# The first layer's attention as one stream of 64 head pairs, with scores formed twice and banks of their own for each use

## What is computed

```python
x = x + layernorm(attn(layernorm(x)))          # 32 heads of 16, one shared key/value head
x = x + layernorm(layernorm(x) @ W.T + bias)   # 512 x 512, W dequantised

q = (h @ Wq).reshape(b, s, 32, 16)
k, v = (h @ Wkv)[..., :16], (h @ Wkv)[..., 16:]
scores = einsum('bqhd,bkd->bhqk', q, k) * 0.25 + slopes[h] * (pos[k] - pos[q])
attn = softmax(where(k <= q, scores, -inf))
out = einsum('bhqk,bkd->bqhd', attn, v).reshape(b, s, 512) @ Wo
```

## Time and profile before

| what | value |
|---|---|
| median of 3 runs | 2521.51 us (2521.39 to 2526.22) |
| the profiled execution's own time | 2520.12 us |
| its span, first to last instruction | 2518.3 us |
| busy in the span: PE, DVE, ACT, POOL | 85%, 74%, 61%, 27% |
| granted TensorE clock, mean | 0.94 |
| the first layer in the span | from 59 us to 824 us |
| before it: weights' preparation | 0 to 59 us |
| after it: the second layer | 824 to 2518 us |

### The profile page before, as it was taken

How to read it: one execution, slowest core, us unless ns; L and a number is a source line. 1 busy time by engine, 2 the same in 40 slices (tenths; PEclk the granted TensorE clock), 3 DMA queues, 4 the chain that set the end, 5 groups by cost and what they waited for, 6 DMA issues and landing times. The chain is left out here.

```text
span 2518.3 us, 49756 instructions
## 1 busy us (share of the span) xinstructions
PE 2146.9 (85%) x18352; PEld 1310.3 (52%) x18352; DVE 1864.5 (74%) x4645; ACT 1531.5 (61%) x3606; POOL 688.4 (27%) x563
## 2 busy tenths in 40 slices
PE   6688777778774589999999999999999999758997
PEld 2465555555552255555555555655555556423443
DVE  3688897897995477777777777777777777575554
ACT  2587776777771376667667676667666767341221
POOL 0312212111110243343433343334333333112221
PEclk9899899889997799999999999999999999978999
DMA  5101001000000343444334434443344333320000
GB/s 203 33 2 35 1 7 47 2 18 18 2 18 17 115 81 63 89 87 91 80 66 89 81 71 82 80 91 78 64 89 84 66 68 65 72 87 17 34 17 34
DMA packets 380593, 147.59 MB, mean 59 GB/s; under 512 B 354928, under 2 KB 359664, under 8 KB 378304
## 3 DMA queue, kind: packets, MB, share of 16 engines
q1 hardware_dynamic: 380352, 144.41, 25.5%
HBM read 48.95 MB, written 11.53 MB: 24 GB/s over the span
## 5 line engine op out<-in xcount | busy, mean ns | idle before, releaser
L1157 ACT ACTIVATE xp<-xp,nm 128x128 f32<-128x128 f32 (+3 forms) x512 | 281.3, 550 | 354.5 <-DVE nm L1236 354.5
L1017 POOL TENSOR_TENSOR q_in_sbuf<-q_in_sbuf,sinq 128x512 f32<-128x512 f32 x128 | 231.2, 1806 | 688.2 <-ACT q_in_sbuf L1145 581.3
L1207 DVE SCALAR_TENSOR_TENSOR probs_lo<-xp,rl,probs_hi 128x128 f16<-128x128 f32 (+3 forms) x512 | 263.5, 576 | 109.4 <-ACT probs_hi L1122 109.4
L575 ACT ACTIVATE xp<-xp,nm 128x512 f32<-128x512 f32 (+3 forms) x512 | 249.8, 569 | 50.9 <-DVE nm L680 49.1
L680 DVE CUSTOM_DVE_ANT_0 xp<-bank,tab,cs 128x512 f32<-128x512 f32 (+3 forms) x512 | 250.2, 545 | 4.3 <-PE bank L459 2.0
L1236 DVE CUSTOM_DVE_ANT_0 xp<-bank,mask,cs 128x128 f32<-128x128 f32 (+3 forms) x512 | 250.3, 545 | 0.0
L1122 ACT ACTIVATE probs_hi<-xp,rl 128x128 f16<-128x128 f32 (+3 forms) x512 | 244.0, 549 | 0.7 <-DVE rl L1256 0.7
L472 PE MATMUL bank<-ident,xp 128*128 128x128 f32 x1280 | 182.7, 291 | 62.6 <-ACT xp L575 45.6
L1041 PE MATMUL bank<-xT_hi,wq_hi 128*128 128x512 f16 x512 | 195.2, 381 | 43.2 <-DVE yacc L1251 37.4
L708 DVE TENSOR_TENSOR pT_lo<-bank,pT_hi 128x384 f16<-128x384 f32 (+1 forms) x384 | 207.1, 593 | 32.5 <-ACT pT_hi L543 32.4
L1041 PE MATMUL bank<-p1T_hi,v_hi 128*128 128x128 f16 x1280 | 223.0, 220 | 2.9 <-DMA p1T_lo<-probs_lo 2.9
(11 more groups left out here) (235 smaller groups left out, 5535.9 us busy)
## 6 DMA issues: line engine op xcount, KB each, us to landing
raw_q<-in_wq SPq DMA_DIRECT2D x8, 1024.0 KB, 5.3
raw_o<-in_wo SPq DMA_DIRECT2D x8, 1024.0 KB, 5.6
x_front<-in_x SPq DMA_DIRECT2D x4, 1024.0 KB, 5.8
xb<-in_x SPq DMA_DIRECT2D x4, 1024.0 KB, 7.1
x_scratch<-xb SPq DMA_DIRECT2D x4, 1024.0 KB, 4.4
x_before<-x_scratch SPq DMA_DIRECT2D x4, 1024.0 KB, 5.6
wup<-in_wup SPq DMA_DIRECT2D x3, 1024.0 KB, 11.9
fused_scratch<-fused SPq DMA_DIRECT2D x12, 256.0 KB, 2.4
```

The source lines that it names most:

```text
L575: act.activation(x, x, ACT.Exp, scale=-1.0, bias=nm[:, h % 4, t:t + 1]).then_inc(s_ex, 1)
L1017: pool.tensor_tensor(qs[:, i % 2, :], qs[:, i % 2, :], rope["sink" if u[0] == "k" else "sinq"][:, :], ALU.mult).then_inc(s_rot, 1)
L1157: ins = act.activation(x, x, ACT.Exp, scale=-1.0, bias=nm[:, m % 3, t:t + 1], accum_out=ls[:, m % 3, t:t + 1])
L1207: ins = dve.scalar_tensor_tensor(pr[1][:, m % 2, c], xp[:, m % 3, c], rl[:, m % 3, t:t + 1], pr[0][:, m % 2, c], ALU.mult, ALU.subtract)
```

## The change

`layer0` becomes one block without barriers: a list of steps, one per pair of heads, for all 64 pairs of the four batches (`STEPS`). Step n of each engine forms the scores of pair n, the exponents of pair n - 6, weighs the values of pair n - 8 and norms the heads of pair n - 9; `FRONT` and `BACK` say at which steps of a batch its input norm, its projections and its back end are done.

- The scores are formed twice on PE. Once with queries in the partitions (`scores`, banks 0 to 2), of which DVE only takes the maximum (`maximise`, five `tensor_reduce` of 512 columns per pair). The second time with keys in the partitions (`exponents`, banks 3 to 5), so that the weights need no transposes. Slopes times positions and minus the maxima are extra rows of the stacked operands (`qs`, `ks`), and the mask is a small product (`far` x `tri`) added to each diagonal tile.
- ACT takes the exponential from PSUM to `px`, five instructions of 512 columns per pair. POOL makes the high halves of the five blocks (`weights_hi`, L487, a cast) and the low halves of two blocks; DVE makes the low halves of three (`weights_lo`, L888). All of these read SBUF, no longer PSUM.
- The queries' stacks are made by SP with 24 DMAs for each group of four pairs (`stack_queries`), the maxima's rows with 4 DMAs (`stack_maxima`).
- A head's output is summed and divided on POOL (`norm_heads`, four small instructions per pair). The normalised rows are made on ACT (`normalise`), the additions of the residual on POOL (`add_rows`), whose `rstd` has two more instructions.
- All other uses share banks 6 and 7. The tables `sel` and `pairmask` are no longer loaded.

The core of the diff (the new functions of POOL and of DVE; the removed lines are those printed above):

```diff
+        STEPS = range(-20, NP + N_LAG + 26)
+        FRONT = {"load": -16, "norm": -11, "n1": (-8, -7), "V": -6, "K": -5}
+        BACK = {"load": 27, "o": (14, 17, 21, 26), "y": (28, 28, 29, 29), "add1": 30, "n2": (32, 34),
+                "f": (36, 36, 38, 38), "add2": 39, "n3": (46, 47)}
...
+        groups = {"s": banks[0:3], "x": banks[3:6], "rest": banks[6:8]}
...
+                def rstd(i):
+                    pool.wait_ge(s_ve, i + 1)
...
+                    pool.tensor_tensor(rs[:, :], ve[:, :], C["mhalf"][:, 0:TT], ALU.pow).then_inc(s_pw, 1)
+                    pool.wait_ge(s_pw, 2 * i + 1)
+                    pool.tensor_tensor(nb[:, :], mv[:, :, 0], rs[:, :], ALU.mult).then_inc(s_pw, 1)
+                    pool.wait_ge(s_pw, 2 * i + 2)
+                    pool.tensor_scalar(nb[:, :], nb[:, :], -1.0, None, ALU.mult).then_inc(s_rs, 1)
...
+                def weights_hi(p):
+                    if p >= 2:
+                        pool.wait_ge(s_pf, p - 1)
+                    for i, (c0, c1) in enumerate(((0, 2), (2, 4), (4, 5))):
+                        pool.wait_ge(*emptied[("x", p, c1 - 1)])
+                        pool.tensor_copy(ph[0][:, p % 2, c0:c1, :], px[:, p % 2, c0:c1, :]).then_inc(s_wh, 1)
+                    pool.wait_ge(s_wh, 3 * p + 3)
+                    pool.tensor_tensor(ph[1][:, p % 2, 3:5, :], px[:, p % 2, 3:5, :], ph[0][:, p % 2, 3:5, :],
+                                       ALU.subtract).then_inc(s_wc, 1)
...
+                for n in STEPS:
+                    if 0 <= n - X_LAG < NP:
+                        weights_hi(n - X_LAG)
+                    if 0 <= n - N_LAG < NP:
+                        norm_heads(n - N_LAG)
+                    for u in norms_at(n):
+                        rstd(norm_no[u])
+                        if u in add_no:
+                            add_rows(u)
...
+                def turn(n, *which):
+                    for i in which:
+                        if 0 <= n < NP:
+                            scores(n, i)
+                        if 0 <= n - X_LAG < NP:
+                            exponents(n - X_LAG, i)
...
+                    for u in norms_at(n):
+                        normalise(u)
...
+                def weights_lo(p, i):
+                    c = slice(2 * i, 2 * i + 2 - i)
+                    dve.wait_ge(s_wh, 3 * p + i + 1)
...
+                    dve.tensor_tensor(ph[1][:, p % 2, c, :], px[:, p % 2, c, :], ph[0][:, p % 2, c, :],
+                                      ALU.subtract).then_inc(s_wl, 1)
```

More of the change, by code:

```diff
@@ new lines, in layer0 @@
+        kk = [sc.sb("k_hi", [P, S], F16), sc.sb("k_lo", [P, S], F16)]
+        kb = sc.sb("k_both", [P, 2, S], F16)
+        kz = sc.sb("k_stack_max", [P, 2, 2, S], F16)
+        ks = sc.sb("k_stack", [P, 2, 2, S], F16)
+        posr = sc.sb("position_rows", [P, S], F16)
+        v2 = sc.sb("v2", [P, 2, TT, 2 * EV], F16)
+        px = sc.sb("weights", [P, 2, 5, S])
+        ph = [sc.sb("weights_hi", [P, 2, 5, S], F16), sc.sb("weights_lo", [P, 2, 5, S], F16)]
+        pos = px[:, 1, 0, :]
+        sl = px[:, 1, 1, 0:H0]
@@ new lines, in layer0 @@
+        s_vd = sc.sem("s_values_out")
+        s_qf = sc.sem("s_queries_filled")
+        s_qh = sc.sem("s_queries_hi")
+        s_qd = sc.sem("s_queries_out")
+        s_qs = [sc.sem(f"s_queries_stacked{i}") for i in range(2)]
+        s_sf = sc.sem("s_scores_filled")
+        s_sd = sc.sem("s_scores_maximised")
+        s_mx = sc.sem("s_maxima")
+        s_mf = sc.sem("s_maxima_transposed")
+        s_mh = sc.sem("s_maxima_hi")
+        s_md = sc.sem("s_maxima_out")
+        s_mr = [sc.sem(f"s_maxima_stacked{i}") for i in range(2)]
@@ L251, in layer0 @@
+        s_ff = sc.sem("s_f_filled")
+        s_fd = sc.sem("s_f_out")
         s_out = sc.sem("s_x_stored")
[L253 to L269, removed]
@@ new lines, in layer0 @@
+        fillings = {"s": [], "x": [], "rest": []}
+        for n in STEPS:
+            if 0 <= n < NP:
+                fillings["s"] += [("s", n, i) for i in range(5)]
+            if 0 <= n - X_LAG < NP:
+                fillings["x"] += [("x", n - X_LAG, i) for i in range(5)]
+            if 0 <= n - V_LAG < NP:
+                fillings["rest"].append(("pv", n - V_LAG))
+            if n % GP == 0 and 0 <= n // GP - 1 < NG:
+                fillings["rest"].append(("m", n // GP - 1))
+            fillings["rest"] += others(n)
@@ new lines, in layer0, with bank_of @@
+        for u in fillings["s"] + fillings["x"] + fillings["rest"]:
+            full, empty = signals[u[0]]
+            counted[full] = counted.get(full, 0) + 1
+            filled[u], emptied[u] = (full, counted[full]), (empty, counted[full])
+        def bank_of(u):
+            k, i = place[u]
+            return groups[k][i % len(groups[k])]
+        norms, adds = [], []
+        for n in STEPS:
+            for kind, when in (("n1", FRONT["norm"]), ("a1", BACK["add1"]), ("n2", BACK["add1"] + 1),
+                               ("a2", BACK["add2"]), ("n3", BACK["add2"] + 1)):
+                if at(n, when) is not None:
+                    norms.append((kind, at(n, when)))
+                    if kind in ("a1", "a2"):
+                        adds.append((kind, at(n, when)))
@@ new lines, in statistics, with variance @@
+                def statistics(t, src):
+                    ch.tick(dve.bn_stats(st[:, int(src is xf), t, :], src[:, t, :]))
+                def variance(u):
+                    if norm_no[u]:
+                        dve.wait_ge(s_nm, TT * norm_no[u])
+                    ch.settle()
+                    for t in range(TT):
+                        ch.tick(dve.bn_aggr(mv[:, t, :], st[:, int(u[0] == "n1"), t, :]))
+                    ch.settle()
+                    dve.tensor_scalar(ve[:, :], mv[:, :, 1], EPS, None, ALU.add).then_inc(s_ve, 1)
```

998 lines of the change are left out of this document (558 added, 440 removed).

## The result

The changed kernel takes 2558.1 us in the median of four runs (2555.0 to 2566.2), the kernel before 2522.3: a ratio of 1.0145, 95% interval 1.0122 to 1.0167. It is slower, by 36 us. The forecast was slower by 100, that is 2620 us, with a range of 2430 to 2740. The profiled execution of the change is the longest of its four (2566.2 us, span 2564.4), so between the two profiled executions there are 46 us to explain.

The account below looks back on a forecast made before the run. POOL, with the time of the port it shares with DVE, was taken to bind: 131 start + 627 pairs + 100 batch work + 66 end = 924 us against 824, so 2620 us from 2520.1; range 2430 to 2740.

Parts of the forecast that it names:

- POOL with gaps in which it waits for ACT's exponentials: Sign that the forecast is wrong: POOL would stand idle for ACT's exponentials, or for PE's sums.
- POOL over 85% busy: Sign that the forecast is right, in the layer's middle: POOL busy or waiting for itself or for DVE's low halves.
- A plain pair: Pair of heads without per-batch work: 8.2 us of POOL plus 1.6 of port, 9.8 us; 64 of them 627.
- Where it waits for its own last instruction, 0.25 us pass: POOL's waits for itself: five of eight instructions 1.2 us, the other starts 0.25 together, per pair.
- POOL's work per batch: Five rstd 10 us, residual additions 12.4, norms 11: together 33 us per batch, 100 for three batches.
- the bubble at the norms: Three norms per batch where ACT waits for POOL, then makes rows and exponentials before POOL's next cast: 3.7 us each.
- Start: Layer's beginning: stack of queries ready at 107 to 112, then six scores-only steps; POOL starts at 131 us.
- 3.3 us each: Time of each of the first six steps, which form scores only, before POOL starts.
- 6 us: Layer's end: the last pair's way through DVE, PE, ACT and DVE to POOL, before a back end of 60 us.
- POOL is cheap and DVE binds: Rival: POOL's pair costs 6.5 us, DVE binds at 8.2 per pair, kernel faster at 2418 us; chance 0.26.
- Small instructions are dear: Rival: POOL's small instructions near 1.02 us, norm_heads 2.7 us more per pair, kernel at 2793 us; chance 0.12.
- The port costs nothing: Rival: the shared port's time is nothing or falls into waits, 102 us less, 2518 us, no change; chance 0.12.

Follow-up runs that it names:

- Experiment 3: Changed kernel with ACT's normalised rows and POOL's residual additions one step later, and n2, n3 too: 2500.3 us, ratio 0.9903 to the kernel before.
- experiment 12: Changed kernel with 12 of the first query stack's 24 DMAs issued by ACT's queue: 2557.4 us, ratio 1.0117 to the kernel before.
- experiment 1: Changed kernel with DVE's low halves replaced by one-input reductions of the same columns, leaving out three blocks' low halves: 2508.0 us, ratio 0.9938 to the kernel before.
- experiment 2: Changed kernel with the low half of one block on POOL instead of two, four on DVE: 2538.6 us, ratio 1.0062 to the kernel before.

## Why the prediction was wrong in size

For the plain pair the side and the mechanism were right: POOL binds, DVE has room, the port's time lies on POOL. For the rest they were not. The prediction wrote down "POOL with gaps in which it waits for ACT's exponentials" and PE's low clock as signs that it is wrong, and both are there: 116.5 us of such gaps, and a clock of 0.50 in the keys' step. Of its signs of being right, POOL over 85% busy became 78%, DVE under 75% became 76%, and DVE waits for `weights_hi` for 10.6 us in all. The size was 2.2 times too large by the profiled executions (100 against 46 us), 2.8 times by the medians (36). By steps:

- **A plain pair, 9.8 us foreseen, 7.55 measured; 144 us too much over 64.** The step that failed most is "Where it waits for its own last instruction, 0.25 us pass", five times a pair and 0.25 more for other starts: 1.45 us. In the plain step above, POOL's instructions follow one another within 0.08 us or overlap: 0.1 us in place of 1.45, which is 87 of the 144 us. The 0.26 of the earlier trace rows is the gap between two instructions of the second layer, 512 columns each; it was the only such row I took, and it isn't the price of a wait for oneself in general (even behind the power of a norm the gap is 0.07). Why it is longer there, no run shows. The rest: casts 2.69 for 3.1 (512 columns 0.605, not the table's 0.70; the fixed part, 2 x 0.605 less 1.04, is 0.17 where 0.2 was taken), the low half 2.12 for 2.35, small instructions 1.2 for 1.3, the port 1.45 for 1.6. Measured parts: 2.69 + 2.12 + 1.2 + 1.45 and 0.1 of gaps are 7.55.
- **POOL's work per batch, 100 foreseen, 150 measured** (633 less 64 x 7.55). The prediction had the bubble at the norms as 3.7 us each; it is 7.7 where the rows above show it, because ACT loses its lead and POOL waits at the two next casts too. Experiment 3 takes most of this away and with it 58 us. Nothing was priced for the steps in which DVE makes the next keys: two of them last 17.7 us, PE stands 5.55 us behind DVE, and its clock falls to its lower level.
- **Start, 131 foreseen, 147 measured.** The steps that failed are "3.3 us each" for the six steps of scores alone, and a smaller one ahead of them. The first scores started at 114.8, where the stack was to be ready at 107 to 112: the first query's low half came at 97.6, not 93, and the 24 issues then took 0.63 us each, near the upper end of the prediction's 0.4 to 0.67 (experiment 12). From the first maxima to POOL's first cast 31.9 us pass, 5.3 for each of six steps. DVE's reductions there are 34, about 22 us, 3.7 a step, and between them DVE waits for PE's products, which I had priced at nothing:

```profile
L874 DVE TENSOR_REDUCE mx<-bank 128x1 f32<-128x512 f32 x14 | 8.9, 679 | 12.2 <-PE bank L544 12.2
```

- **End, 66 foreseen, 86 measured.** The step that failed first is "6 us" for the last pair's way to POOL's normed heads. They were finished 14.3 us after the last low half, at 794.5, because POOL, in order, made an `rstd` and the four residual additions of the batch before ahead of them, and PE stood 11.02 us for them:

```profile
788.23 4.93 POOL L499 TENSOR_TENSOR xb<-xb,yb 128x512 f32<-128x512 f32 x4 [0.93 <-ACT yb L707]
794.60 1.11 PE L588 MATMUL bank<-ident,heads_normed 128*128 128x128 f32 x4 [11.02 <-POOL heads_normed L478]
```

  That is 8 of the 20 us. In experiment 3, where `rstd` stands among the heads and the additions behind them, the same way takes 7.5 us (727.65 to 735.2). In the change ACT also makes that norm's four rows, 2.93 us, before it copies the heads' transposes. The other 12 us aren't divided by an experiment; PE's clock over the stretch is 0.69.
- **The rivals.** "POOL is cheap and DVE binds" put its bound at 8.2 us for POOL's pair and would have had the change faster. POOL came to 7.55, under that bound, and the kernel is still slower: the rival's start and end were as far off as mine, and it had nothing for the long steps. "Small instructions are dear" is out (0.295). "The port costs nothing" is out by experiment 1. That it put the time at no change, 36 us from what was measured, would have been an accident of other terms.

The sum of the four: -144 + 50 + 16 + 20 = -58 of the layer, and +4 of the second: 100 - 54 = 46. Two errors of opposite sign, each larger than the answer of 46 itself, stood in a forecast whose direction was right. The range held the measured time for that reason, by luck and not by its working. Taking nine of the eleven long steps away without touching POOL's work is what turns the change into a gain (2500 us).

The Trainium skill, SBUF — State Buffer, section on who interferes with whom, has a DVE instruction with two SBUF inputs and a GpSimd one that reads SBUF locking each other out for the whole instruction. The timeline of the plain step and experiment 1 agree: 1.4 us per plain pair, 50 us in all.

## What to carry to other kernels

Price a step of an engine that takes over work as the sum of its instructions alone and measure the gaps between them from neighbours of the same kind, not behind one odd instruction. Then look at the steps that are not plain: an in-order engine that waits for a result made at the end of its partner's step loses its lead over that partner, and a delay of one step at that point was worth more (58 us) than moving a block of work from one engine to another (19 us). Where two engines share a port, moving a block from one to the other gives back part of what it takes, so a split is worth little near the balance.

## What the runs showed of the hardware

- A cast from f32 to f16 on POOL takes 1.04 us for 1024 columns and 0.605 for 512; two inputs of 1024 columns take 2.12, and 64 columns 0.295. For casts and for two inputs these figures give 0.17 to 0.18 us per instruction beside the columns, an estimate (2 x 0.605 less 1.04, and 2 x 1.15 of experiment 2 less 2.12). A chain of instructions on POOL that wait for each other has gaps of about 0.08 us.
- The port passes between DVE and POOL at the ends of instructions. A short POOL instruction behind a DVE one takes 0.75 us instead of 0.30, and the cast of 512 columns just before the plain step above 1.60 instead of 0.605. What an instruction pays is what is left of the other engine's, not a share of its own length.
- The clock's price shows in two products of the same form, behind PE's wait of 5.55 us and 5 us later:

```profile
335.51 0.63 PE L524 MATMUL bank<-wo_hi,heads_T_lo 128*128 128x512 f16 x1
335.94 0.63 PE L524 MATMUL bank<-wo_lo,heads_T_hi 128*128 128x512 f16 x1
...
340.13 0.38 PE L524 MATMUL bank<-wo_hi,heads_T_lo 128*128 128x512 f16 x1
340.34 0.38 PE L524 MATMUL bank<-wo_lo,heads_T_hi 128*128 128x512 f16 x1
```

From start to start they take 0.43 us at a clock of 0.50, and 0.21 where it is 0.97 again: a wait of PE is paid once more in the products behind it.
